# Layernorm scales moved from GpSimd to ScalarE, eight buffers for the broadcast rows, new step numbers, written-out loops and finer waits in a two-layer kernel on Trainium2

## The reference, cut to what matters

```python
h = _layernorm(x) * (1 + ca) + sa                  # ln "a"
x = x + ga * gated_linear_attention(h)             # layer 0, chunks of 64 tokens
h = _layernorm(x) * (1 + cb) + sb                  # ln "b"
x = x + gb * per_channel_mlp(h)
h = _layernorm(x) * (1 + ca) + sa                  # ln "c"
x = x + ga * state_space(h)                        # layer 1: for each of 16 states
#   state_t = state_{t-1} * (1 - dt_t * k_t^2) + (x_t * dt_t) * k_t ;  y_t = sum_n state_t * q_t
h = _layernorm(x) * (1 + cb) + sb                  # ln "d"
x = x + gb * experts(h)                            # 8 experts, each takes its 512 best
#   tokens of each of the 2 batches: gelu(h @ w1) @ w2, scaled by the gate, scattered back
```

## Time and profile before

| | us |
|---|---|
| median of 3 runs | 2094.49 (2094.24 to 2097.22) |
| the profiled execution: its time | 2097.58 |
| the profiled execution: span from first to last instruction | 2095.4 |
| PE busy | 1771.5 (85% of the span) |
| DVE busy | 1569.0 (75%) |
| POOL busy | 1439.5 (69%) |
| ACT busy | 1301.9 (62%) |

### The profile page before, as it was taken

One profiled execution on the slowest core, in us unless ns is written; L12 is line 12 of the kernel. 1 busy time (PEld: TensorE's weight loads), 2 busy tenths in 40 slices (PEclk: granted clock), 3 DMA queues, 4 the chain that ended last, 5 costly groups with the idle time before them and its releaser, 6 DMA issues. The chain is left out here.

```text
span 2095.4 us, 40115 instructions
## 1 busy us (share of the span) xinstructions
PE 1771.5 (85%) x12344; PEld 1521.1 (73%) x12344; DVE 1569.0 (75%) x3158; ACT 1301.9 (62%) x2316; POOL 1439.5 (69%) x836
## 2 busy tenths in 40 slices
PE   5578998989989899898998989988662499999996
PEld 5456887877878778787887878876551388888886
DVE  3336898887978888888888888987646777777772
ACT  0257787776867777777777777876321255555552
POOL 0005899998989989899898999999970244343342
PEclk9788999999999999999999999999875599999998
DMA  4001332223223233322322222223211233333321
GB/s 167 15 1 47 68 67 60 65 58 76 62 56 64 59 75 56 64 65 57 76 55 65 63 59 76 60 64 61 69 39 57 71 79 81 77 81 75 76 45 21
DMA packets 110368, 132.78 MB, mean 63 GB/s; under 512 B 7969, under 2 KB 103073, under 8 KB 109985
## 3 DMA queue, kind: packets, MB, share of 16 engines
q1 hardware_dynamic: 97680, 113.04, 22.3%
q0 software_dynamic: 12288, 16.79, 4.4%
q10 hardware_dynamic: 272, 1.57, 0.2%
HBM read 105.68 MB, written 17.30 MB: 59 GB/s over the span
## 5 line engine op out<-in xcount | busy, mean ns | idle before, releaser
L1071 DVE TENSOR_TENSOR_SCAN st<-pD,last,st 128x256 f32<-128x256 f32 x1024 | 693.9, 732 | 136.3 <-PE pD L1022 114.3
L1090 POOL TENSOR_TENSOR st<-u,kqb 128x1024 f32<-128x1024 f32 x256 | 605.0, 2363 | 85.2 <-DMA kqb<-kq_rows 76.1
L1080 POOL TENSOR_TENSOR sq<-st,kqb 128x1024 f32<-128x1024 f32 x256 | 605.0, 2363 | 26.9 <-DVE st L1071 22.5
L1052 ACT ACTIVATE decT<-ndT,ones_s,kkT 128x512 f32 (+1 forms) x512 | 407.4, 806 | 81.5 <-PE pD L1022 72.6
L1039 PE MATMUL pY<-ident_s,sq 128*128 128x128 f32 x2048 | 324.6, 283 | 62.1 <-POOL sq L1080 62.0
L1022 PE MATMUL pD<-ident_s,decT 128*128 128x128 f32 x2048 | 326.2, 284 | 53.7 <-DVE st L1071 48.3
L1022 PEld LDWEIGHTS pD<-ident_s,decT 128*128 128x128 f32 x2048 | 251.3, 146 | 108.8 <-DVE st L1071 61.6
L1039 PEld LDWEIGHTS pY<-ident_s,sq 128*128 128x128 f32 x2048 | 247.3, 145 | 81.8 <-POOL sq L1080 77.5
L1805 POOL DMA_INDIRECT y_out<-ys,ids x64 | 108.6, 1698 | 247.1 <-DVE ys L1632 150.4
L1750 PE MATMUL po<-w_up,h_up 128*128 128x256 f32 x512 | 147.8, 289 | 19.9 <-DVE h_rest L1593 19.0
L1750 PE MATMUL po<-w_rest,h_up 128*128 128x256 f32 x512 | 145.5, 284 | 0.0
(11 more groups left out here) (269 smaller groups left out, 3756.3 us busy)
## 6 DMA issues: line engine op xcount, KB each, us to landing
kqb<-kq_rows SPq DMA_DIRECT2D x256, 256.0 KB, 4.6
w_in<-w_d SPq DMA_DIRECT2D x16, 1024.0 KB
ndT<-ndS SPq DMA_DIRECT2D x16, 512.0 KB, 3.4
xt<-x_in SPq DMA_DIRECT2D x16, 256.0 KB, 2.8
y_out<-xo SPq DMA_DIRECT2D x16, 256.0 KB, 4.8
xn_rows<-xnC SPq DMA_DIRECT2D x16, 256.0 KB, 2.1
W<-weights SPq DMA_DIRECT2D x1, 3505.5 KB, 21.9
wmod<-wmod ACTq DMA_DIRECT2D x1, 1536.0 KB, 11.0
```

Source lines behind the costliest of these rows:

```text
L1052: act.activation(decT[:, m % 2, t, :], turn2(ndT, it, NT * DI, t * DI, DI), ACT.Identity, bias=ones_s[:, 0:1], scale=turn2(kkT, it, NT * D ...
L1071: dve.tensor_tensor_scan(run, pD[h][:, k2 * TB:(k2 + 1) * TB], run, last[:, bass.ds(later(it) * (DS * DT) + m * DT + k, 1)], ALU.mult, ALU ...
L1080: pool.tensor_tensor(sq[:, m % 2], st[:, m % 4], kqb[:, m % SLOTS, 1, :].unsqueeze(1).broadcast_to([P, DT, TB]), ALU.mult).then_inc(sem("r ...
L1090: pool.tensor_tensor(st[:, m % 4], turn2(u, it, DT * TB).rearrange("p (k t) -> p k t", k=DT), kqb[:, m % SLOTS, 0, :].unsqueeze(1).broadca ...
```

## The change

It has six parts, and the arithmetic is the same.

1. `ln_pool` and its three small POOL instructions are gone, as is the add of 1e-5 on DVE. `ln_scale` on ACT takes their place: Ln(var + eps), minus mean, Exp(-0.5 * that), and two products of one column each, five small activations with two waits on ACT itself, four times a turn.
2. `SLOTS` goes from 4 to 8.
3. Every step number in `AT` is chosen anew.
4. The loop of turns 3 to 13 is written out, and so are those of the experts (`every_turn`, SP's loop over experts, ACT's over weight quarters).
5. In `experts`, the down matmuls of a list wait chunk by chunk for the split of the hidden values, and no longer for all 8 chunks.
6. The up matmuls wait for the half of the next expert's weights that belongs to w1, and the other half is waited for ahead of the down matmuls.

```diff
-SLOTS = 4
+SLOTS = 8
 AT = dict(
-    stat_a=3, ln_a=19, rows_a=2, turn_a=7, mod_a=4, low=7, v=18, lr=10, v_s=14, z=22, abs=21, exl=21, gk=26, G0=30,
+    stat_a=0, ln_a=2, rows_a=4, turn_a=6, mod_a=7, low=8, v=17, lr=14, v_s=17, z=21, abs=21, exl=23, gk=27, G0=27,
...
-            dve.wait_ge(sem(f"ln{n}_var"), it * 2 + 1)
-            dve.tensor_scalar(ve[n][:, :], mv[n][:, :, 1], EPS, None, ALU.add).then_inc(sem(f"ln{n}_var"), 1)
-
-        def ln_pool(pool, it, n):
-            pool.wait_ge(sem(f"ln{n}_var"), it * 2 + 2)
-            pool.wait_ge(sem(f"ln{n}_rows"), it)
-            pool.tensor_tensor(nm[n][:, :], mv[n][:, :, 0], minus[:, :], ALU.mult)
-            pool.tensor_tensor(rstd[n][:, :], ve[n][:, :], expo[:, :], ALU.pow).then_inc(sem(f"ln{n}_rstd"), 1)
-            pool.wait_ge(sem(f"ln{n}_rstd"), it * 2 + 1)
-            pool.tensor_tensor(nmr[n][:, :], nm[n][:, :], rstd[n][:, :], ALU.mult).then_inc(sem(f"ln{n}_rstd"), 1)
+
+        def ln_scale(act, it, n):
+            act.wait_ge(sem(f"ln{n}_var"), it + 1)
+            act.activation(rstd[n][:, :], mv[n][:, :, 1], ACT.Ln, bias=epst[:, :]).then_inc(sem(f"ln{n}_rstd"), 1)
+            act.activation(nm[n][:, :], mv[n][:, :, 0], ACT.Copy, scale=-1.0)
+            act.wait_ge(sem(f"ln{n}_rstd"), it * 3 + 1)
+            act.activation(rstd[n][:, :], rstd[n][:, :], ACT.Exp, scale=-0.5).then_inc(sem(f"ln{n}_rstd"), 1)
+            act.wait_ge(sem(f"ln{n}_rstd"), it * 3 + 2)
+            for t in range(NT):
+                i = act.activation(nmr[n][:, t:t + 1], nm[n][:, t:t + 1], ACT.Copy, scale=rstd[n][:, t:t + 1])
+            i.then_inc(sem(f"ln{n}_rstd"), 1)
...
-            with eng.Fori(3, NB - 2) as i:
+            for i in range(3, NB - 2):
                 a_turn(eng, i, "AFSCG")
...
-            with eng.Fori(1, ITEMS) as i:
+            for i in range(1, ITEMS):
                 a_turn(eng, i, True)
...
-                def in_parts(to, chunks, stationary, moving):
-
-                    terms = [(c, parts) for c in range(chunks) for parts in ((upper, upper), (upper, rest), (rest, upper))]
-                    for n, (c, (p0, p1)) in enumerate(terms):
-                        m = pe.matmul(to, stationary(c, p0), moving(c, p1),
-                                      start=(n == 0), stop=(n == len(terms) - 1))
+                def in_parts(to, chunks, stationary, moving, before=None):
+
+                    for c in range(chunks):
+                        if before is not None:
+                            before(c)
+                        for n, (p0, p1) in enumerate(((upper, upper), (upper, rest), (rest, upper))):
+                            m = pe.matmul(to, stationary(c, p0), moving(c, p1),
+                                          start=(c == 0 and n == 0), stop=(c == chunks - 1 and n == 2))
                     return m
...
+                        expert = (i - 1) * 2 + e2
                         if b == 0:
-                            pe.wait_ge(sem("w_split"), (i - 1) * 2 * WQ + (e2 + 1) * WQ)
-                        pe.wait_ge(sem("upper"), splits(i, n, ahead))
+                            pe.wait_ge(sem("w_split"), expert * WQ + (WQ // 2 if expert else WQ))
+                        before_it = ahead or n < 3
+                        pe.wait_ge(sem("upper"), splits(i, n, ahead) - (WQ // 2 if before_it and expert + b else 0))
...
-                        pe.wait_ge(sem("h1_split"), i * 4 * FT + (n + 1) * FT)
-                        pe.wait_ge(sem("upper"), splits(i, n, ahead) + FT)
+                        if b == 0:
+                            pe.wait_ge(sem("w_split"), (expert + 1) * WQ)
+
+                        def hidden_chunk(f):
+                            pe.wait_ge(sem("h1_split"), i * 4 * FT + n * FT + f + 1)
+                            pe.wait_ge(sem("upper"), splits(i, n, ahead) + f + 1)
```

More of the change, by code:

```diff
@@ L46 @@
 XBUF = 4
-SLOTS = 4
+SLOTS = 8
 STEPS = 64
 AT = dict(
-    stat_a=3, ln_a=19, rows_a=2, turn_a=7, mod_a=4, low=7, v=18, lr=10, v_s=14, z=22, abs=21, exl=21, gk=26, G0=30,
[L56 to L64, removed]
+    stat_a=0, ln_a=2, rows_a=4, turn_a=6, mod_a=7, low=8, v=17, lr=14, v_s=17, z=21, abs=21, exl=23, gk=27, G0=27,
+    G1=28, eG0=25, eG1=27, D0=29, D1=30, eD0=28, eD1=29, q0=31, k0=33, queries0=36, keys0=36, sc0=39, kgt0=38,
+    scored0=42, kv0=42, q1=44, queries1=45, states0=51, k1=48, keys1=51, sc1=54, kgt1=54, scored1=53, kv1=55, g=58,
+    sg=59, states1=57, S0=27, o=59, o_sq=60, ms=61, o_n=61, rms=65, og=66, wo=67, x_attn=4, ln_b=6, rows_b=6,
+    turn_b=8, mod_b=8, win=13, s_f=13, relu0=17, relu1=24, facc0=23, facc1=28, wout=29, x_ffn=30, ln_c=31,
+    rows_c=33, turn_c=35, mod_c=34, halo=38, inx0=38, xcp0=38, inx1=43, xcp1=44, tail=45, conv0=43, conv1=47,
+    xs0=45, xs1=46, inz0=50, sz0=46, dkq_mm=50, dkq=52, inz1=51, sz1=52, kturn=53, kk=53, dt0=53, dt1=55, sig0=54,
+    sig1=56, den=57, nd=60, ut=61, u=69, yz0=19, yz1=19, yt0=21, yT0=20, yt1=22, yT1=22, out=25, x_scan=28, ln_d=40,
+    rows_d=42, turn_d=74, mod_d=75, score=79, scores=81, dec=11, sum=22, open0=21, open1=24, dec_t=6, saved=21,
+    scan=13, rd=23, inp=14)
 PER_BLOCK = dict(
@@ L78 @@
 PER_BLOCK.update({f"ln{n}_{what}": 1 for n in "abcd" for what in ("rows", "stats")})
[L79 to L80 removed]
+PER_BLOCK.update({f"ln{n}_var": 1 for n in "abcd"})
+PER_BLOCK.update({f"ln{n}_rstd": 3 for n in "abcd"})
 PER_BLOCK.update({f"kq_in{slot}": DS // SLOTS * 16 for slot in range(SLOTS)})
@@ L1456, in _ @@
                 load(0)
-                with sp.Fori(1, E) as e:
+                for e in range(1, E):
                     sp.wait_ge(sem("w_split"), e * WQ)
@@ L1691, in a_turn @@
                                             ring(n, FT + DC + q))
-                with act.Fori(0, WQ) as q:
+                for q in range(WQ):
                     act.wait_ge(sem("masked"), q + 1)
@@ L1777, in a_turn @@
                                          lambda f, part: part(h1_up, h1_rest)[:, f, s * P:(s + 1) * P],
-                                         lambda f, part: part(w_up, w_rest)[:, e2, 1, f * D:(f + 1) * D])
+                                         lambda f, part: part(w_up, w_rest)[:, e2, 1, f * D:(f + 1) * D],
+                                         before=hidden_chunk if s == 0 else None)
                             m.then_inc(sem("down_mm"), 1)
```

32 lines of the change are left out of this document (9 added, 23 removed).

## The result

The changed kernel takes 1979.49 us in the median of 4 runs (1977.75 to 1980.56), the kernel before 2095.85 (4 runs): a ratio of 0.9442, with a 95% interval of 0.9426 to 0.9458. The forecast was 2001.5, with a range of 1945 to 2060. The profiled execution has a time of 1979.35 and a span of 1977.6.

What follows compares the result with a forecast made beforehand. Bound: a ring of in-order engines waiting for each other, a turn nearest PE's busy 80.9 us. Fourteen turns 64, last two blocks 6 and experts 23 make 93 us off 2094.5: 2001.5, range 1945 to 2060.

Steps and rivals of the forecast that it cites:

- 14 turns: Layers before the last two blocks: each turn falls by 4.6 us, from 87.9 to 83.3, 64 us in all.
- experts: Expert lists: PE's waits of 19.0 and 6.4 us go, 2.4 comes back; 23 us together, bounds 15 and 31.
- Sum for a turn, on PE: Layer turn on PE: 6.2 us of waits gone, 1.6 new, so 83.3 us; PE's busy time taken as 80.9.
- The new wait: PE's transpose of xnB, now closer behind the wo_g matmuls: at least 1.3, perhaps 2 us a turn, 1.6 taken.
- `ve_a`: DVE's add of EPS in the layernorm, where PE waits for DVE: removing it is worth 0.92 us a turn.
- The issue gap: DVE standing still ahead of u behind the loop's branch: 1.87 us a turn, gone once the loop is written out.
- POOL: relief: POOL loses 4.5 us of layernorm work and up to 5.6 of kqb waits a turn; 1.5 off PE's wait.
- The long wait: POOL's wait for the kqb transfer at state 10, behind the write of xnC: stays possible, 0 to 4 us.
- The order on PE: PE's new order in a turn: 1.29 us for hA and 0.58 for kgt go; a wait for xnB comes.
- A: Rival: POOL's relief is taken up by the ring of engines; turn 86.5 us, time 2045; chance 0.22.
- B: Rival: PE is no bound, the new order packs it until POOL sets the pace; turn 79.5, time 1947; chance 0.10.
- C: Rival: slower, ACT's layernorm waits for DVE's statistics with decT queued behind; turn 92.1 us, time 2124; chance 0.08.

Runs made afterwards that it cites:

- e4: The kernel before with only the layernorm's scale moved to ACT, directly ahead of its rows, old steps and four slots; ratio 0.9821 to the kernel before.
- g2: The kernel before with the layernorm's scale on ACT at the old steps and the layers' loop written out; ratio 0.9711 to the kernel before.
- g3: The changed kernel with the step numbers of the kernel before; ratio 0.9509 to the kernel before, 14 us slower than the changed kernel.
- e1: The kernel before with only the loop over the layers' middle turns written out; ratio 0.9881 to the kernel before, 25 us faster.
- e3: The kernel before with only eight slots for kqb in place of four; ratio 1.0056 to the kernel before, 12 us slower.
- f1: The changed kernel with the layers' middle turns in a loop again; ratio 0.9816 to the kernel before, 78 us slower than the changed kernel.
- f2: The changed kernel with four slots for kqb again; ratio 0.9691 to the kernel before, 52 us slower than the changed kernel.
- f3: The changed kernel with the layernorm's scale back on POOL and the EPS add on DVE, at the new steps; ratio 1.0435 to the kernel before.
- g1: The changed kernel with the layernorm's scale on POOL and the EPS add on DVE, with layernorm steps chosen for POOL; ratio 0.9915 to the kernel before.
- g4: The changed kernel with the back projection's group of 8 matmul calls issued twice; ratio 0.9693 to the kernel before, 52 us slower than the changed kernel.

## Why the prediction was right, and where it was not

The forecast was a gain of 93 us and the kernel gained 117; its time lies inside the stated range. The profiled spans are 117.8 us apart. They divide as follows, in us.

| | forecast | measured |
|---|---|---|
| 14 turns | 64 | 76.0 |
| last two blocks | 6 | 9.5 |
| start and end | 0 | -1.1 |
| experts | 23 | 33.5 |

**PE's idle time in a turn: right in sum.** Forecast: 6.2 gone, 1.6 new, 4.6 less. Measured: 7.0 to 2.7, 4.3 less. `hA` and `kgt` went as forecast (1.87) and the wait for `sq` went whole (1.8, forecast 1.5). The wait for DVE's scan went from 3.25 to 1.9 us a turn, where the sum took 2.8 off it, and 0.6 for `dkq` and `og` are new.

**The turn: 83.3 forecast, 81.5 measured.** The step that failed is the end of "Sum for a turn, on PE", which took PE's busy time, 80.9, as given. It fell by 2.0. The granted clock is part of it: with almost the same matmuls, the turns of e4, g2, g3 and the changed kernel ran at 1.00 in the mean, and those of before, e1, e3, f1, f2, f3 and g1 at 0.95 to 0.99, and e1 gives the price: 2.5 us more of busy time in a turn at 0.96. The clock is not all of it: one turn of before (928.54 to 1016.48 us) shows 1.00 and still 80.2 busy. The rest may be matmuls drawn out by waits in between; that isn't separated. For the experts the prediction had put the clock into its bounds, for the layers it had not.

**Fourteen turns: two errors that oppose each other.** The sum takes what a steady turn gives 14 times. Ten blocks gave 6.6 us each, more than the 4.6 forecast, and the other four 2.6 each. The loop's gap is not in those four: in e1 they are as long as in the kernel before (331.9 us against 333.2). With the right value of a steady turn the term would have been 90 us or more where 76.0 were measured. So part of its nearness is luck.

**The new wait: other place, a little smaller.** It was forecast as 1.6 us at the transpose of `xnB` and is a wait of 1.64 at the scan's bank. DVE has the add, the statistics, a pair of scans and `u` in line there, and PE needs a bank from the next scan before it comes to `xnB`, whose rows are ready in the meantime. Some wait at the bank was there with the old steps too: 8.1 us in g3 against 19.0 now, so the new steps added 1.1 us a turn. (The working's lower bound has a slip: three times 0.93 are 2.8 us for the six groups, not 2.6, so 1.1 and not 1.3.)

**`ve_a`: put into a wait that it stands behind.** The 0.92 us were taken off PE's wait of 2.92 us. That wait ends with the scan of 956.34 us, and `ve_a` begins at 959.35, so it can only delay the pair of scans behind it. PE waited for those in few turns: the earlier trace rows has 12 waits in ten turns, ten of them the large one. The reading of 0.92 as 0.17 of work and 0.75 of waiting for POOL holds, as the adds under g1 show. It held for the other three adds too, which the sum left out: together they took 2.9 us of DVE a turn, not 0.92.

**The issue gap: gone as forecast, but not by one part only.** 1.87 us a turn fits e1, where PE's idle time fell by 2.0; but there are 11 such turns and not 14 (25 us are 2.3 for each of them, clock included). And "it goes with the loop" hid two things: the scale on ACT removes the gap with the loop in place (e4), and behind the new steps the loop would cost 78 us (f1).

**POOL: relief right, its worth not.** The sum took 1.5 us off PE's wait for `sq` "since POOL speeds up", for kqb and layernorm together. e3 shows that the `kqb` waits by themselves were worth nothing: waits for DVE took their place. It was the layernorm: in e4, with four slots, PE's wait for `sq` is down to 0.4 us a turn. The long wait stays as bounded: 2.35 us once a turn.

**ACT: right.** 69.7 busy a turn, forecast 70.4; `Ln` takes 0.285 and each `nmr` 0.287 us where 0.197 was taken, but those within one layernorm overlap (0.48 for two `nmr`). Five table loads each, as before.

**The order on PE: net 0.3 forecast, 0.9 measured.** The forecast gave it 1.87 us a turn for `hA` and `kgt` and charged 1.6 for the new wait; g3 has 0.9 between the two orders. There the wait for `hA` is back and that for `kgt` is not, so the order was not what took the latter.

**Experts: 23 forecast, 33.5 measured, outside the bounds of 15 to 31.** The failed step is the same as in the turn. PE's idle time fell by 21.9 us (27.1 to 5.2), near the 23: the waits of the earlier trace rows are gone, and 4.5 us for `ys`, six times, came where 2.4 were given back. PE's busy time, again taken as given, fell by 11.6 (394.3 to 382.7). Fewer falls of the clock are part of that. By runs, the waits brought 26.5 and the written-out loops, priced at nothing, 7.

**Its own signs.** No gap ahead of `u`, no wait of `po` for `h_rest` and ACT near 70 came as named. Three did not: POOL waits 2.35 us a turn for `kqb` (named: under 2), the turn is 81.5 (near 83), and PE's largest wait is not at `xnB`.

**The rivals.** A (the waits move, 86.5) did not come. B ended on the right side: the turn, 81.5, lies halfway between its 79.5 and the forecast. But its ground, that PE is no bound, falls: g4 added 3.45 us to PE's matmul time and the turn grew by 3.5. The Trainium skill ("Perfetto Trace Analysis", on identifying the most-contended engine) calls matmul busy time a poor measure of how near TensorE is to its roofline. g4 does not test that, since the added group brings weight loads as well; it tests what sets the pace. C asked for waits of `decT` behind ACT's layernorm; the largest, `rstd_b` for its variance, is 10.1 us in the whole run.

## What to carry to other kernels

A part's worth is not a property of the part. Alone, the loop gave 25 us, the slots lost 12, the scale on ACT gave 37 and the experts' part 35, 85 together, while the whole, with the new steps, gave 117. Taken out of the finished kernel the loop and the slots were worth 78 and 52, and the steps 14. Step numbers fit one assignment of work to engines; when work moves to another in-order queue, give it new ones before judging the move (f3 against g1). Before crediting a wait's removal, ask what else stands in that queue: by the traces the buffers for `kqb` paid through the copy of `ndS` behind them. And a bounding engine's busy time is not a constant: here waits taken from PE gave back part of its matmul time too, in the layers and in the experts.

## What the runs showed of the hardware

- Writing out the loop took 2.0 us of PE's idle time off a turn in one order of the same work and is worth 5.2 in another (holes in DVE's sequencer of 3.2 and 5.3 us up to its next register instruction), while ACT's branch in f1 at 682.0 was followed by its next register instruction within 0.3 us.
- The granted clock moved with small amounts of waiting on PE: 1.00 throughout the steady turns of g3, the changed kernel and g4, with 2.7 to 3.4 us of PE idle a turn; 0.97 in f2, with 4.4. The amount alone does not decide it, since e4, with 4.3, is at 1.00; PE's longest single wait from 400 to 1216 us is 1.4 us in e4, 1.6 in the changed kernel and g4, 2.8 in f2 and 3.3 in the kernel before. g4 and f2 have turns of about the same length, 85.0 and 84.9 us; PE is busy 82.3 of them in g4 and 80.5 in f2. In e1 a turn at 0.96 had PE busy 81.3 us and one at 1.00 78.9, for the same 594 matmuls.
- DVE's add on 128x2 took 0.17 us, but when it began during a POOL instruction it ended, 46 times in the kernel before, 0.02 to 0.03 us behind the end of that instruction, 1.7 us after its own start at the most.
- An activation of 128x1 with a scale from SBUF takes 0.287 us and a pair 0.48; with a constant scale 128x2 takes 0.19 (Copy) and 0.20 (Exp).
